# The last sequence of an attention stage: order of the down-row reads, PSUM banks, division and Silu table

## Chip, cores and metric

The kernel runs on one core of one Trainium2 chip. The metric is device microseconds for one execution of the whole program. PE is the tensor engine (TensorE), PEld its weight loads, ACT is ScalarE, DVE is VectorE, POOL is GpSimd, SP is the engine that here only issues DMAs.

## What is computed

x has 16 sequences of 256 tokens with 256 channels. Four blocks follow, each added to its input after a layer norm: causal attention with 16 heads, a feed-forward stage whose weights are rebuilt from spline control points, a gated linear attention, and the feed-forward stage again.

```python
x = x + attn_a(layernorm(x), Wq, Wk, Wv, Wo)        # 16 heads of 16, causal softmax
x = x + ffn(layernorm(x), gate_cp, up_cp, down_cp)  # down(silu(gate(x)) * up(x)), 1024 inner
x = x + attn_b(layernorm(x), Wq, Wk, Wog, Wig, g)   # gated linear attention
x = x + ffn(layernorm(x), gate_cp, up_cp, down_cp)
```

The change lies in the first block's last sequences and the first rows of the first feed-forward stage.

## The kernel before

Everything is fp32 kept as a high and a low part, so a projection is three matmuls (`mm3`, L414 to L416). Each engine has its own program, written out by hand, and runs it strictly in order; engines meet only at semaphores. `upto(s, b, k)` is the count that semaphore s has when step k of sequence b is done.

**Attention** runs in periods, one for each sequence b = 0 to 15. A period has eight steps p, each for a pair of heads. In step p PE makes the shifted scores of b (`shifted`, L870, into the double bank `pair_a`), then the plain scores of b + 1 (`scores` and `hide_future`, L839 and L851, into `pair_b`), of which DVE takes maxima (L1689). ACT takes the exponential (`exps`, L1314) from `pair_a`, POOL masks it (L660), and every second step PE weighs V with it (`weigh`, L884 and L888). `shifted(b, u, p)` waits until the exponential of step p - 1 has read `pair_a`.

The maxima become two rows of the operand that `shifted` reads: `turn_max` (PE, L858), `split_max` (DVE, L1702, L1704), and `max_rows(b, u, h)` (SP, L505), four DMAs of 4 KB, once for steps 0 to 3 (h = 0) and once for steps 4 to 7 (h = 1). `stack_half` (SP, L497), six DMAs of 128 KB, brings the other rows of a later sequence. The rest of a period finishes sequence b - 1: `turn_o` (L897), `divide` (DVE, L1711 and L1715), `turn_att` (L905), `copy_att` and `low_att` (L1326, L1722), `proj_out` and `residual` (L1728).

**The feed-forward stage (FFN)** works on eight groups of 512 tokens. For each group DVE takes statistics (L1829), ACT normalises into `xr` (L1433), PE turns it (`f1_turn`, two calls a group, L1071), ACT and DVE write high and low parts to `fs` (`f1_high_x` L1439, `f1_low_x` L1848), moments follow (`f1_moments`, `f1_high_moments` L1444, `f1_low_moments` L1853). SP stores these to `fx` in device memory (`f1_write_x`, four DMAs, `f1_write_moments`, two; L557 and L559) and reads them back in another layout to `stk` (`f1_read`, eight DMAs, L578). Then come eight steps m: gate (L1103) into `pair_a`, up (L1106) into `pair_b`, Silu on ACT (L1449), the product on DVE (`gated`, L1860), and from m = 3 on the down matmuls of step m - 3.

The first three groups' inputs are prepared inside attention's last periods. In the last period (b = 15) there are no scores of b + 1, so `pair_b` is free: the turns of groups 1 and 2 and the moments of group 1 use it. FFN group 0 also carries the end of sequence 15 (`last_attention`): turn_o at m = 0, division and turn_att at m = 1, proj_out at m = 2.

The **down weights** come from `wdx` in device memory by 16 DMAs (`load_down`, L526), eight in period 14 after `max_rows(14, 1)` and eight at its very end after the fx stores. In period 15 ACT makes their high part (`high_down`, L1362) and DVE the low part (`low_down`, L1823) in steps 2, 4, 6 and 7. All DMAs of SP are issued in the order of its program. Its period before:

```python
max_rows(b, u, 1)
if nxt2: stack_half(b + 2, u, 0)
if nxt and not nxt2: load_down(range(KG // 2))      # b = 14
if nxt: max_rows(b + 1, 1 - u, 0)
if nxt2: stack_half(b + 2, u, 1)
if nxt and not nxt2:                                # b = 14
    f1_write_x(0, 0); f1_write_moments(0, 0)
    load_down(range(KG // 2, KG))
```

`nxt`, `nxt2`, `nxt3` say whether sequences b + 1, b + 2, b + 3 exist.

## Time and profile before

| | us |
|---|---|
| median of three runs | 854.33 |
| their range | 853.58 to 856.82 |
| the profiled execution's span | 855.9 |
| PE, weight loads busy | 781.1, 661.1 |
| DVE, ACT, POOL busy | 629.3, 495.2, 236.7 |

No other time of the profiled execution is given than its span, the time from its first to its last instruction. The page cuts the span into 40 slices of 21.4 us; attention is slices 3 to 17, and the last sequence and the start of the FFN lie in slices 17 to 19, where PE has an 8 and the granted clock an 8. A row of a window gives its length, the busy us (and instructions) of PE, PEld, DVE, ACT and POOL, the granted clock, the busy share of the 16 DMA engines and GB/s. A window's granted clock is a mean: 1.00 is 2.4 GHz, 0.50 is 1.2 GHz. In a timeline the number in brackets is the idle time of the engine before the instruction, with what released it. PE's row of a matmul counts its modelled end, so starts are the better measure of its pace.

### The profile page before, as it was taken

What the parts mean: (1) busy time and instruction counts of PE and PEld (TensorE: products, weight loads), DVE (VectorE), ACT (ScalarE), POOL (GpSimd) and SP (SyncE); (2) the same over time, 40 slices, a digit from 0 to 9 for tenths busy, and PEclk for the clock granted to TensorE, in tenths of its full rate; (3) what the DMA queues carried; (4) which work ended last, traced back from release to release, by engine and by line L of the source; (5) the groups of instructions that cost most, each with busy time, mean ns of one, the idle gap of its engine ahead of it and who ended that gap; (6) DMA issues with size and microseconds to landing.
All of it is one profiled execution on the core that took longest, in us unless ns stands there. A gap on an engine that the chain in (4) does not pass through costs nothing.

```text
span 855.9 us, 19706 instructions
## 1 busy us (share of the span) xinstructions
PE 781.1 (91%) x6676; PEld 661.1 (77%) x6676; DVE 629.3 (74%) x1272; ACT 495.2 (58%) x967; POOL 236.7 (28%) x306
## 2 busy tenths in 40 slices
PE   4789899999999999869999999999999869999998
PEld 3667677777777777648889888888888849898887
DVE  7466777777777777736888767689887647887755
ACT  3146455555455556565666657588887736666643
POOL 2932223322323332311001001166666451000000
PEclk9669999999999999968999999999999988999999
DMA  5945766666666655575666640000033134777741
GB/s 182 112 79 79 147 89 97 97 94 90 88 95 97 96 87 78 159 262 174 254 237 233 243 163 2 1 2 1 1 134 149 37 120 162 256 257 272 263 156 50
DMA packets 70960, 111.16 MB, mean 130 GB/s; under 512 B 7061, under 2 KB 27958, under 8 KB 70854
## 3 DMA queue, kind: packets, MB, share of 16 engines
q1 hardware_dynamic: 70896, 110.35, 50.6%
q8 instruction: 35, 0.57, 0.3%
q14 instruction: 29, 0.24, 0.1%
HBM read 41.82 MB, written 42.81 MB: 99 GB/s over the span
## 4 chain that ended last, share of the span: by engine, by line
PE 48%; DVE 16%; issue 9%; ACT 8%; DMA 7%; SPq 7%; POOL 4%; ACTq 0%; DVEq 0%; POOLq 0%
PE bank L414 7%; PE bank L415 6%; PE bank L416 6%; DMA stk<-fx 5%; PE pair_a L870 4%; DVE inter L1860 4%; PE bank L884 4%; PE pair_b L839 3%; SPq L578 3%; PE pair_a L1156 2%; ACT in_hi L1457 2%; DVE in_lo L1865 2%; DVE spline L1937 2%; ACT gact L1449 2%; ACT xr L1433 2%
## 5 line engine op out<-in xcount | busy, mean ns | idle before, releaser
L414 PE MATMUL bank<-wd_hi,in_hi 128*128 128x256 f32 x512 | 146.4, 286 | 2.0 <-DVE X L1871 1.7
L416 PE MATMUL bank<-wd_hi,in_lo 128*128 128x256 f32 x512 | 145.5, 284 | 0.0
L415 PE MATMUL bank<-wd_lo,in_hi 128*128 128x256 f32 x512 | 145.3, 284 | 0.0
L1314 ACT ACTIVATE prob<-pair_a 128x768 f32<-128x768 f32 x128 | 103.7, 810 | 66.5 <-PE pair_a L870 65.5
L660 POOL TENSOR_SCALAR_AFFINE_SELECT prob<-prob 128x512 f32<-128x512 f32 x128 | 82.1, 641 | 212.8 <-ACT prob L1314 212.8
L1457 ACT ACTIVATE in_hi<-inter 128x512 fp32r<-128x512 f32 x128 | 80.7, 630 | 103.2 <-DVE inter L1860 97.6
L1865 DVE TENSOR_TENSOR in_lo<-inter,in_hi 128x512 fp32r<-128x512 f32 x128 | 89.0, 696 | 64.8 <-ACT in_hi L1457 63.4
L1689 DVE TENSOR_REDUCE mx<-pair_b 128x6 f32<-128x768 f32 x124 | 118.0, 952 | 24.1 <-PE pair_b L851 23.1
L414 PEld LDWEIGHTS bank<-wd_hi,in_hi 128*128 128x128 f32 x512 | 97.8, 191 | 7.1 <-issue 2.3
L415 PEld LDWEIGHTS bank<-wd_lo,in_hi 128*128 128x128 f32 x512 | 97.5, 190 | 4.8
L416 PEld LDWEIGHTS bank<-wd_hi,in_lo 128*128 128x128 f32 x512 | 97.5, 190 | 0.0
L1860 DVE TENSOR_TENSOR inter<-gact,pair_b 128x512 f32<-128x512 f32 x128 | 87.0, 680 | 6.3 <-ACT gact L1449 4.8
L1449 ACT ACTIVATE gact<-pair_a 128x512 f32<-128x512 f32 x128 | 74.5, 582 | 5.9 <-PE pair_a L1103 5.9
L870 PE MATMUL pair_a<-stack 50*128 50x256 f32 x512 | 66.6, 339 | 11.7 <-ACT prob L1314 7.7
L870 PEld LDWEIGHTS pair_a<-stack 50*128 50x128 f32 x512 | 39.8, 191 | 37.3 <-issue 14.8
L1103 PE MATMUL pair_a<-stk,cst 126*128 126x512 f32 x128 | 52.9, 413 | 11.2 <-DMA stk<-fx 6.1
L839 PE MATMUL pair_b<-stack 48*128 48x256 f32 x496 | 56.2, 304 | 5.2 <-DVE mx L1689 2.4
L712 POOL TENSOR_TENSOR frs<-fve,half_neg 128x4 f32<-128x4 f32 x16 | 16.1, 1008 | 144.2 <-DVE fve L1839 144.2
L1106 PE MATMUL pair_b<-stk,cst 126*128 126x512 f32 x128 | 53.9, 421 | 1.5 <-DVE inter L1860 1.5
L1302 ACT ACTIVATE stage<-bank 128x512 fp32r<-128x512 f32 x32 | 19.2, 599 | 56.2 <-PE bank L416 53.2
L839 PEld LDWEIGHTS pair_b<-stack 48*128 48x128 f32 x496 | 39.3, 192 | 12.5 <-DVE mx L1689 7.6
L884 PE MATMUL bank<-prob,V 128*32 128x256 f32 x512 | 42.7, 406 | 0.1
(226 smaller groups left out, 1960.9 us busy)
## 6 DMA issues: line engine op xcount, KB each, us to landing
stk<-fx SPq DMA_DIRECT2D x128, 252.0 KB
stack<-stage SPq DMA_DIRECT2D x192, 128.0 KB, 4.7
fx<-fs SPq DMA_DIRECT2D x32, 512.0 KB, 3.5
fx<-fs SPq DMA_DIRECT2D x32, 256.0 KB, 3.7
fx<-fs SPq DMA_DIRECT2D x16, 504.0 KB
fx<-fs SPq DMA_DIRECT2D x16, 252.0 KB
X<-in_attn_a_x SPq DMA_DIRECT2D x14, 256.0 KB, 5.0
result<-X SPq DMA_DIRECT2D x7, 512.0 KB, 8.1
```

The costliest lines, as they stand in the source:

```text
L414: pe.matmul(dst, l_hi, r_hi, start=first, stop=False)
L415: pe.matmul(dst, l_hi, r_lo, start=False, stop=False)
L416: return pe.matmul(dst, l_lo, r_hi, start=False, stop=last)
L660: pool.affine_select(out=diag, in_=diag, compare_op=ALU.is_ge, fill=0.0, base=0, pattern=[[0, 2], [0, 2], [1, P]], channel_multiplier=-1). ...
L839: pe.matmul(dst[:, n, at_col:at_col + S], stack[rows, u, h, p % PR, 0, P * t:P * t + P], stack[rows, u, h, p % PR, 1, :], start=(t == 1), ...
L870: i = pe.matmul(pair_a[:, n, at_col:at_col + S], stack[rows, u, h, p % PR, 1, P * t:P * t + P], stack[rows, u, h, p % PR, 0, :], start=Tru ...
L1314: act.activation(prob[:, p % 4], pair_a[:, :, P:4 * P], ACT.Exp, scale=DK ** -0.5).then_inc(a_e, 1)
L1449: act.activation(gact[:, m % 2, :], pair_a[:, m % 2, :], ACT.Silu).then_inc(f_.si, 1)
L1457: act.activation(in_hi[:, m % LAG, :], inter[:, m % 2, :], ACT.Copy).then_inc(f_.ih, 1)
L1689: dve.tensor_reduce(mx[:, h, :, p % PR, :], src[:, :, 0:3 * P].rearrange("p n (t k) -> p n t k", t=3), AX.X, ALU.max).then_inc(a_mx, 1)
L1860: dve.tensor_tensor(inter[:, m % 2, :], gact[:, m % 2, :], pair_b[:, m % 2, :], ALU.mult).then_inc(f_.up, 1)
L1865: dve.tensor_tensor(in_lo[:, m % LAG, :], inter[:, m % 2, :], in_hi[:, m % LAG, :].bitcast(F32), ALU.subtract).then_inc(f_.il, 1)
```

## The change

On SP, the first eight down reads move from period 14 (after `max_rows(14, 1)`) to the end of period 13, ahead of `max_rows(14, 1)`. The second eight, and `f1_write_x(0, 0)`, move ahead of `max_rows(15, 0)`. `f1_write_moments(0, 0)` stays behind it.

In period 15 shifted scores go to `pair_a` in even steps and to `pair_b` in odd ones, and wait only for the exponential of step p - 2. So the turns and moments of groups 1 and 2 leave `pair_b` for single banks (`bank_y`, `bank_p`, `bank_t`) at steps 0, 3 and 5, each with waits for the bank's former reader. `high_down` moves from ACT to DVE, both down parts at steps 2 to 5. ACT runs a Silu of one element a partition right after the last exponential, which loads Silu's table there. `divide(15, 1)` moves from m = 1 to m = 0 of FFN group 0, ahead of the first `gated`.

```diff
 (SP, period)
                 if nxt and not nxt2:
-                    load_down(range(KG // 2))
+                    load_down(range(KG // 2, KG))
+                    f1_write_x(0, 0)
                 if nxt:
                     max_rows(b + 1, 1 - u, 0)
                 if nxt2:
                     stack_half(b + 2, u, 1)
+                if nxt2 and not nxt3 and b == B - 3:
+                    load_down(range(KG // 2))
...
                 if nxt and not nxt2:
-                    f1_write_x(0, 0)
                     f1_write_moments(0, 0)
-                    load_down(range(KG // 2, KG))
 (PE, shifted)
-                pe.wait_ge(a_e, upto(a_e, b, p))
+                last = isinstance(b, int) and b == B - 1
+                pe.wait_ge(a_e, upto(a_e, b, p - 1 if last and p else p))
+                dst = pair_b if last and p % 2 else pair_a
 (PE, period)
+                    if p == 0 and not nxt:
+                        pe.wait_ge(a_mx, upto(a_mx, B - 1, NP))
                     shifted(b, u, p)
...
                     if p == 2 and prev:
                         pe.wait_ge(a_at, upto(a_at, b - 1, 1))
+                        if not nxt:
+                            pe.wait_ge(f_.xl, upto(f_.xl, 1, 1))
                         turn_o(b - 1, 1)
...
                         elif nxt:
                             pe.wait_ge(f_.ml, upto(f_.ml, 0, 1))
+                        else:
+                            pe.wait_ge(f_.xl, upto(f_.xl, 2, CT))
                         pe.wait_ge(a_res, upto(a_res, b - 2, 1))
                         proj_out(b - 1)
                     if not nxt:
                         if p == 0:
-                            pe.wait_ge(a_mx, upto(a_mx, B - 1, NP))
-                        if p in (1, 5):
-                            if p == 5:
-                                pe.wait_ge(f_.ml, upto(f_.ml, 1, 1))
-                            for c in range(CT):
-                                f1_turn(1 + p // 4, c, pair_b[:, c, :])
+                            pe.wait_ge(a_at, upto(a_at, B - 2, 1))
+                            f1_turn(1, 0, bank_y)
+                            pe.wait_ge(a_res, upto(a_res, B - 3, 1))
+                            f1_turn(1, 1, bank_p)
                         if p == 3:
-                            f1_moments(1, pair_b[:, 0, :])
+                            f1_moments(1, bank_p)
+                        if p == 5:
+                            pe.wait_ge(a_atl, upto(a_atl, B - 2, 1))
+                            f1_turn(2, 0, bank_t)
+                            pe.wait_ge(f_.ml, upto(f_.ml, 1, 1))
+                            f1_turn(2, 1, bank_p)
 (ACT, period)
                     exps(b, p)
+                    if p == NP - 1 and not nxt:
+                        act.activation(silu_first[:, :], quarter[:, :], ACT.Silu)
...
-                        if p in (1, 7):
-                            for c in range(CT):
-                                f1_high_x(1 + p // 4, c, pair_b[:, c, :])
-                        if p == 3:
-                            f1_high_moments(1, pair_b[:, 0, :])
+                        if p == 1:
+                            f1_high_x(1, 0, bank_y)
+                            f1_high_x(1, 1, bank_p)
                         if p == 4:
                             f1_normalise(2)
-                        if p in (2, 4, 6, 7):
-                            high_down((p - 1) // 2)
+                        if p == 6:
+                            f1_high_x(2, 0, bank_t)
+                            f1_high_x(2, 1, bank_p)
...
                             copy_att(b - 1)
+                        if not nxt:
+                            f1_high_moments(1, bank_p)
 (DVE, period; low parts of groups 1 and 2 at p = 1, 3, 6 in the same banks)
-                        if p in (2, 4, 6, 7):
-                            low_down((p - 1) // 2)
+                        if p in (2, 3, 4, 5):
+                            high_down(p - 2)
+                            low_down(p - 2)
 (DVE)
+            def high_down(n):
+                dve.wait_ge(s_wd, 256)
+                rows = slice(2 * n, 2 * n + 2)
+                dve.tensor_copy(wd_hi[:, rows, :], wd_lo[:, rows, :].bitcast(F32)).then_inc(s_wdh, 1)
 (DVE, last_attention)
-                if m == 1:
+                if m == 0:
                     divide(B - 1, 1)
```

## Rows read from the trace of the kernel before

**Rows 1.** Windows: each engine's busy us (instructions), granted clock, DMA share, GB/s.

```profile
364.00:366.00 2.00, 0.00 (x0) 0.00 (x0) 0.00 (x0) 0.58 (x2) 0.00 (x0) 1.00 0.26 93
366.00:368.00 2.00, 1.11 (x8) 0.73 (x12) 0.94 (x2) 2.00 (x5) 0.64 (x1) 0.69 1.01 378
380.00:382.00 2.00, 1.33 (x15) 0.72 (x8) 1.89 (x4) 1.23 (x2) 0.00 (x0) 0.90 0.58 226
386.00:388.00 2.00, 0.59 (x4) 0.18 (x2) 2.00 (x5) 1.60 (x3) 0.00 (x0) 0.81 0.61 169
```

**Rows 2.** Timeline of PE: start, us, line, tiles, count, idle before; last sequence.

```profile
353.89 0.50 PE L870 MATMUL pair_a<-stack 50*128 50x256 f32 x4
...
354.77 0.40 PE L888 MATMUL bank<-prob,V 128*32 128x128 f32 x8
...
356.04 1.04 PE L1071 MATMUL pair_b<-ident,xr 128*128 128x128 f32 x8
...
366.89 0.79 PE L870 MATMUL pair_a<-stack 50*128 50x256 f32 x4 [3.21 <-ACT prob L1314]
...
381.34 0.50 PE L1103 MATMUL pair_a<-stk,cst 126*128 126x512 f32 x1 [0.67 <-DVE fs L1848]
```

**Rows 3.** Timeline of ACT, then of DVE; last sequence.

```profile
358.99 1.08 ACT L1439 ACTIVATE fs<-pair_b 128x512 fp32r<-128x512 f32 x2 [2.25 <-DMA fx<-fs]
359.96 0.82 ACT L1314 ACTIVATE prob<-pair_a 128x768 f32<-128x768 f32 x1
365.42 0.63 ACT L1362 ACTIVATE wd_hi<-wd_lo 128x512 fp32r<-128x512 f32 x1 [4.64 <-DMA wd_lo<-wdx]
...
368.43 2.07 ACT L1433 ACTIVATE xr<-X,fnmr,frs 128x256 f32<-128x256 f32 x4
...
381.37 1.28 ACT L1449 ACT_TABLE_LOAD   x1
...
359.62 1.29 DVE L1848 TENSOR_TENSOR fs<-pair_b,fs 128x512 fp32r<-128x512 f32 x2 [2.05 <-ACT fs L1439]
```

**Rows 4.** Timeline of PE's weight loads: shifted(14, 4) and shifted(15, 4).

```profile
342.95 0.30 PEld L870 LDWEIGHTS pair_a<-stack 50*128 50x128 f32 x4 [0.19 <-DMA stack<-mrow]
...
366.86 0.53 PEld L870 LDWEIGHTS pair_a<-stack 50*128 50x128 f32 x4 [3.60 <-DMA stack<-mrow]
```

**Rows 5.** Timeline of SP's queue, issues only; periods 13 to 15.

```profile
333.90 4.89 SPq L497 DMA_DIRECT2D stack<-stage  x6
339.24 2.56 SPq L505 DMA_DIRECT2D stack<-mrow  x4
341.84 2.90 SPq L526 DMA_DIRECT2D wd_lo<-wdx  x8
...
357.44 4.71 SPq L526 DMA_DIRECT2D wd_lo<-wdx  x8
362.20 2.44 SPq L505 DMA_DIRECT2D stack<-mrow  x4
364.75 0.39 SPq L557 DMA_DIRECT2D fx<-fs  x1
```

**Rows 6.** Windows as in rows 1: stack copies, down reads, reads of stk.

```profile
339.00:340.00 1.00, 1.00 (x22) 0.57 (x18) 1.00 (x2) 0.33 (x1) 0.51 (x1) 1.00 1.04 123
347.00:348.00 1.00, 1.00 (x9) 0.81 (x5) 0.63 (x5) 0.67 (x1) 0.17 (x1) 1.00 0.56 76
372.00:373.00 1.00, 1.00 (x7) 0.67 (x5) 0.00 (x0) 0.19 (x1) 0.64 (x1) 0.50 0.58 211
```

**Rows 7.** DMA issues of 325 to 395: count and KB each.

```profile
stk<-fx SPq DMA_DIRECT2D x16, 252.0 KB
...
wd_lo<-wdx SPq DMA_DIRECT2D x16, 64.0 KB
```

**Rows 8.** Timeline of PE: start of the FFN, and its first down matmul.

```profile
385.37 0.66 PE L905 MATMUL bank<-ident,att 128*128 128x128 f32 x4 [2.38 <-DVE att L1715]
...
394.02 0.30 PE L414 MATMUL bank<-wd_hi,in_hi 128*128 128x256 f32 x1
```

More of the change, by code:

```diff
@@ L188, in build @@
         quarter = sb("quarter", [P, 1], F32)
+        silu_first = sb("silu_first", [P, 1], F32)
         cst = sb("cst", [NFX, 2, MT, P], F32R)
@@ L869, in shifted @@
                         rows = slice(HALF * n, HALF * n + K_ST)
-                        i = pe.matmul(pair_a[:, n, at_col:at_col + S], stack[rows, u, h, p % PR, 1, P * t:P * t + P],
+                        i = pe.matmul(dst[:, n, at_col:at_col + S], stack[rows, u, h, p % PR, 1, P * t:P * t + P],
                                       stack[rows, u, h, p % PR, 0, :], start=True, stop=True,
@@ L1264, in _ @@
             weigh(B - 1, 1, NP - 2)
-            pe.wait_ge(f_.xl, upto(f_.xl, 2, CT))
             pe.wait_ge(s_ce, 6)
@@ L1313, in exps @@
                 act.wait_ge(a_pv, upto(a_pv, b, p - 3))
-                act.activation(prob[:, p % 4], pair_a[:, :, P:4 * P], ACT.Exp,
+                src = pair_b if isinstance(b, int) and b == B - 1 and p % 2 else pair_a
+                act.activation(prob[:, p % 4], src[:, :, P:4 * P], ACT.Exp,
                                scale=DK ** -0.5).then_inc(a_e, 1)
@@ L1357, in spread_rows @@
                     act.activation(wdn[:, 0, :, 0:1], wdn[:, 0, :, D:D + 1], ACT.Copy).then_inc(s_wdn, 1)
-            def high_down(n):
-                act.wait_ge(s_wd, 256)
-                rows = slice(2 * n, 2 * n + 2)
-                act.activation(wd_hi[:, rows, :], wd_lo[:, rows, :].bitcast(F32), ACT.Copy).then_inc(s_wdh, 1)
             act.wait_ge(s_const, 5)
@@ L1807, in period @@
                     if not nxt:
-                        if p in (1, 7):
-                            for c in range(CT):
-                                f1_low_x(1 + p // 4, c, pair_b[:, c, :])
-                        if p == 3:
-                            f1_low_moments(1, pair_b[:, 0, :])
                         if p == 0:
                             f1_stats(2)
-                        if p in (2, 4, 6, 7):
-                            low_down((p - 1) // 2)
+                        if p == 1:
+                            f1_low_x(1, 0, bank_y)
+                            f1_low_x(1, 1, bank_p)
+                        if p == 3:
+                            f1_low_moments(1, bank_p)
+                        if p in (2, 3, 4, 5):
+                            high_down(p - 2)
+                            low_down(p - 2)
+                        if p == 6:
+                            f1_low_x(2, 0, bank_t)
+                            f1_low_x(2, 1, bank_p)
             attention = period
+            def high_down(n):
+                dve.wait_ge(s_wd, 256)
+                rows = slice(2 * n, 2 * n + 2)
+                dve.tensor_copy(wd_hi[:, rows, :], wd_lo[:, rows, :].bitcast(F32)).then_inc(s_wdh, 1)
             def low_down(n):
```

## The prediction, on record before the changed kernel was run

> **What bounds the kernel now.** I read the page's slices of the span first: the tensor engine (PE) is nearly always busy in the attention periods and again once the first feed-forward stage (FFN) runs, so little can be won there. The one hole is the last sequence, b = 15, from its first shifted scores at 353.89 to the first gate matmul at 381.34, 27.45 us [rows 2]. Its windows show what goes wrong: PE does nothing at all from 364 to 366, the granted clock is 1.00 until then and 0.69 over the next window, so 0.50, that is 1.2 instead of 2.4 GHz, from about 366.8 on; in 380 to 382 it is 0.90, so it came back at about 380.4 [rows 1]. The timelines of ACT and PE then name the waits. ACT stood 2.25 us for the landing of `f1_write_x(0, 0)` before it could copy the next FFN input, and 4.64 us for the down rows; PE, in order behind the exponentials, stood 3.21 us, and the matmuls after it run at half rate [rows 2, 3]. The third thing is the queue of SP: the rows of maxima (`max_rows`), the down rows and the fx stores share one queue, and `max_rows(14, 1)` is landed only 0.19 us after PE wants it at 342.95 [rows 4]. That one decides this forecast.
>
> **The change part by part.**
>
> *The last sequence on PE, clock at 2.4 GHz; t = 0 is its first shifted scores.* A set of shifted scores and a weighing take 1.28 us together (353.89 to 354.77 + 0.40), which I split 0.43 and 0.85; eight turns take 1.04, one exponential 0.82, two copies to fs 1.08 on ACT and 1.29 on DVE, a normalisation 2.07 [rows 2, 3]. I follow the new order by these. p = 0: shifted(0), weigh, f1_turn(1, 0) and (1, 1), to 2.25. p = 1: shifted(1) goes to pair_b and no longer waits for exps(0); turn_max to 3.1. DVE then writes the maxima's rows by 4.0; exps(1) ends at 3.6, high_x at 4.6, low_x at 5.4. The wait for the fx store is gone, because that store is issued a period earlier. p = 2 to 3: weigh(0) must wait for mask(1) until 4.5, turn_o to 5.9, division on DVE to 6.7, turn_att and the moments to 8.6. p = 4 to 5: shifted, weigh, shifted to 10.3; then PE waits for ACT's normalisation, which ends at 12.2. p = 6 to 7: the turns, shifted, weigh, turn_o to 15.7, shifted(7) to 16.15; proj_out now waits for low_x(2), which stands behind divide(15, 0) on DVE, until 17.7; proj_out and the last weighing end at 20.1. The eight down copies are now on DVE, each pair of copy and subtraction at most 1.35 us (a subtraction of this shape takes half of the 1.29 us above; a copy of it has no row on DVE and lies between nothing and the same): they fill DVE's gap from 6.7 to 14, and cost nothing as long as divide(15, 0) at 15.8 finds DVE free. ACT loses 4 x 0.63 us of copies that were beside PE's waits [rows 3].
>
> *A new wait takes the place of the old ones.* The first gate needs all eight reads of stk. Before, `f1_write_x(1, 1)` was issued at 364.75 and the reads right behind it [rows 5]. They move 8 x 252 KB at 211 GB/s with 0.58 of the DMA engines busy [rows 6, 7], so 9.5 us, behind about 4 us of fx stores; with a little over 1 us at each end that is 15.8 us from the first store to the last landing, and 364.75 + 15.8 = 380.5 was just hidden under the gate at 381.34. Now the store is issued when low_x(1) is done (5.4) and SP is through with `max_rows(15, 1)` (4.05 + 2.44 = 6.5), and 6.5 + 15.8 = 22.3. PE is ready at 20.1, so the gate comes at 22.4. Gain in this stretch: 27.45 - 22.4 = 5.05 us. Bounds: 7.3 (the reads come in time) and 4 (some idle time lowers the clock again).
>
> *The down rows read sooner, and what they are moved past.* Eight reads are now issued at the end of the queue's work of period 13, at 338.8 (333.90 + 4.89), ahead of `max_rows(14, 1)`, which was issued at 339.24 [rows 5]. Their issue alone takes 2.90 us (clear queue) to 4.71 (busy queue), and shifted(14, 4), which wants those rows, stands at the head of PE with everything behind it: a delay of 2.5 us is the least (the old issue at 339.24 becomes 341.7). But the transfers are slower than the issue. In the old order these same eight kept 0.56 of the DMA engines busy and moved 76 GB/s in a window of their stretch [rows 6]: 8 x 64 KB [rows 7] is 6.9 us at that rate. The stretch as a whole, six windows from 343 to 349, is a little faster, so I take 6.1. In the new order they queue behind stack_half(15, 1), which keeps all DMA engines busy in 339 to 340 and ends at about 340.7, so they move until 346.8. If the rows of maxima lie on the same DMA engines in order, they come after: 346.8 + 1.7 = 348.5, that is 5.6 us after 342.95. The upper bound is 6.2 (the queue's slower issues added), the lower 2.5.
>
> The share alone does not say whether the four small rows meet the eight down rows. The Trainium skill ("DMA: Bandwidth & Descriptors", in its part on how many engines k a DMA gets) says that a copy is split over the largest count up to 16 that divides both outer dimensions and that these are the lowest-numbered engines; by that the maxima's four are a part of the down rows' eight, ring order holds, and this speaks against the change: 5.6 us rather than 2.5. No row here names an engine. I take 5.6, because the one place where maxima's rows followed down rows before (issued from 362.20 for 2.44 us) released PE at 366.86, 2.2 us after their last issue against 1.15 us at 342.95 [rows 4, 5]; that is a weak witness, since an exponential ended at about the same time. All of these transfers also lie in the one hardware queue of the page.
>
> *The clock.* PE would be idle from about 342.8 to 348.5. Before, 3.2 us of idle time were enough for a fall to 0.50 [rows 1, 2], so here it falls too, in a stretch in which PE never waits. The fall at 366.8 lasted until 380.4; the next one came at about 387.2 (0.81 in 386 to 388), after a wait of 2.38 us, and was over at 394.02, where a matmul of 256 columns takes 0.30 us [rows 1, 8]. So a fall here lasts 6.8 to 13.6 us. Of the new one, the first 2 us fall on idle time; 4.6 us at half rate cost 2.3 us, 11 cost 5.5. I take 2.5, less 0.4 us of small waits that disappear at half rate. Nothing (no fall) is the other bound.
>
> *Second store moved.* `f1_write_x(0, 0)` and the other eight down reads now stand ahead of `max_rows(15, 0)`. That waits for the maxima of DVE anyway, which come some 8 us later now, and by my count the transfers ahead (6.1 us of reads from 347, then 4 us of stores) end at 357.5, before it lands at 361. Cost nothing; if the cover goes, up to 1 us.
>
> *The start of the FFN.* Division is ahead of the first gated product, and the Silu table (1.28 us) is loaded in ACT's wait for the last weighing [rows 3]. silu(0) comes 0.6 us sooner, but divide (0.7 us) now stands before gated(0), which so starts where it did. turn_att, which PE waited 2.38 us for, is 1.9 us sooner [rows 8]. low_att however keeps its place behind the second pair of statistics on DVE: seven steps at 0.6 us, started 0.6 us sooner. So proj_out comes 0.5 to 0.6 us sooner, not 2. From the gate to the first down matmul took 12.7 us [rows 2, 8], 6.8 of them at half clock; if the clock stays up it is 9.3. Gain 0 to 3.4, I take 0.9, since PE is idle 2.3 us before the gate and 2.5 us before proj_out and the clock probably falls again.
>
> *Sum:* +5.6 + 2.5 - 0.4 - 5.05 - 0.9 = +1.75 us. From the first down matmul on PE is busy almost without a gap and the shift passes to the end. The sum is made against the profiled execution, whose span is 855.9 us, 1.6 over the median of 854.33 and inside the runs shown (853.58 to 856.82); I carry the difference over to the median: 856.1.
>
> **The rivals.**
> *A: the maxima's rows pass the down reads* (other DMA engines, or the issue alone counts). For it: only 0.58 of the engines are busy. Against it: one queue, and the landing in period 15. The stall is 2.5 to 3.7 us and the clock costs 0 to 2.3: the sum is 2.5 + 0 - 5.05 - 3.4 = -6 at best and 3.7 + 2.3 - 0.4 - 5.05 - 0.9 = -0.4 at worst. Time 848.4 to 854, middle 850.5.
> *B, slower: the clock stays down.* After the stall in period 14 PE at 1.2 GHz is given work with many small tiles, as from 366.8 to 380.4, and the clock does not rise before the last sequence starts. Then the clock costs 5.5 us, the steps before 6.5 in the last sequence 1 us more, and the FFN's start gives nothing: 5.6 + 5.5 + 1 - 5.05 = +7, time 861. It decides from about 356: a clock still at 0.50 there is this case.
> *C: the reads of stk come in time after all,* or the change does not shorten the last sequence as said because a DVE wait (divide ahead of low_x) moves the store or the last projection. The first gives 2.3 us more (854), the second 2 us less (858). Both stay within 0.5%.
>
> **How the numbers follow.** Forecast with C: 0.62 (sum from -0.6 to +4). A: 0.22. B: 0.16. 0.5% is 4.3 us, about what a measurement of this kernel can tell from no change. More than that faster is most of A's better half: 0.15. More than that slower is B and an edge of the forecast: 0.20. Within it 0.65. The range leaves out the ends of A and B: 849.5 to 861.0.
>
> **What would show it.** In the profile after: the first down read issued at about 338.8; PE idle before shifted(14, 4) for 5 to 6 us with the release by the maxima's rows, and the clock at 0.50 soon after; the last sequence 22 to 23 us long at full clock with no wait for wd_lo and a wait for stk of about 2 us before the first gate; the table load ended before that gate; turn_att close behind up(1) and proj_out some 6 us after the gate. The forecast is wrong if the wait in period 14 is under 3 us, if the clock does not fall there or stays down, or if the gate does not wait for stk.

## The result, and the profile after

| | median, us | runs shown | ratio to before, 95% interval |
|---|---|---|---|
| before | 856.51 | 853.13 to 860.57 (12) | |
| changed | 861.49 | 858.09 to 868.00 (12) | 1.0068 [1.0044, 1.0093] |

The change costs 5.0 us, 0.7%. The profiled execution took 868.0 us, the longest of the twelve, with a span of 866.3 against 855.9 before. The medians and ratios below leave out a few executions in a slower state of the chip (865.95 and 875.27 us, and three of about 1411).

The difference of the spans must first be cleared of something that has nothing to do with the change. The windows below (length, busy us of PE, PEld, DVE, ACT, POOL, granted clock, DMA share, GB/s) show PE fully busy at 0.50, so at 1.2 GHz, early in attention, where both kernels run the same instructions:

```profile
74.00:86.00 12.00, 12.00 (x78) 9.79 (x77) 2.97 (x5) 6.73 (x17) 1.28 (x2) 0.50 0.44 55
86.00:88.00 2.00, 2.00 (x18) 1.77 (x19) 1.73 (x4) 0.81 (x1) 0.30 (x1) 0.73 0.00 0
```

The trace of before has no such stretch there. With it, period 14 starts at 341.03 instead of 334.89, 6.1 us late. All that follows is therefore measured from the start of period 14, and a time of before is compared after adding 6.1. That the 5.1 us found in this way agree with the 5.0 us of the medians supports the reckoning.

**The stretch that changed.** Times are starts of weight loads in PE's timeline: shifted(14, 0), shifted(14, 4), shifted(15, 0), first gate, first down matmul.

| | (14,0) to (14,4) | to (15,0) | last sequence, to gate | gate to down | all | after it |
|---|---|---|---|---|---|---|
| before | 8.06 | 10.93 | 27.46 | 12.26 | 58.71 | 462.3 |
| changed | 16.97 | 12.90 | 23.08 | 10.90 | 63.85 | 461.4 |
| difference | +8.91 | +1.97 | -4.38 | -1.36 | +5.14 | -0.9 |

The first column is a stall. PE's weight loads in the changed kernel, at shifted(14, 4) and at the first gate (start, us, engine, line, tiles, count, idle time and what ended it):

```profile
358.00 0.50 PEld L874 LDWEIGHTS pair_a<-stack 50*128 50x128 f32 x4 [9.09 <-DMA stack<-mrow]
...
393.98 0.29 PEld L1116 LDWEIGHTS pair_a<-stk,cst 126*128 126x128 f32 x1 [0.38 <-issue]
```

The wait of 0.19 us for the same maxima's rows [rows 4] has become 9.09. At the gate PE now hardly waits. SP's issues in the changed kernel say where the rows stood:

```profile
340.05 4.85 SPq L498 DMA_DIRECT2D stack<-stage  x6
344.94 2.95 SPq L527 DMA_DIRECT2D wd_lo<-wdx  x8
347.94 2.56 SPq L506 DMA_DIRECT2D stack<-mrow  x4
350.55 2.93 SPq L527 DMA_DIRECT2D wd_lo<-wdx  x8
...
377.44 0.39 SPq L559 DMA_DIRECT2D fx<-fs  x1
...
380.12 6.48 SPq L580 DMA_DIRECT2D stk<-fx  x8
```

The rows of (14, 1) were issued by 350.5, 2.6 us later than in [rows 5] once the shift of 6.1 is taken off. The other 6.3 us of the 8.9 are landing: 7.5 us from the end of the issue to PE's start, against 1.15 before. What the DMA engines and the clock did meanwhile, in windows of the changed kernel:

```profile
349.00:353.00 4.00, 0.14 (x2) 0.00 (x0) 1.83 (x5) 0.70 (x2) 0.17 (x1) 1.00 0.57 66
352.00:354.00 2.00, 0.00 (x0) 0.00 (x0) 0.00 (x0) 0.00 (x0) 0.00 (x0) 0.83 0.57 66
354.00:358.00 4.00, 0.00 (x0) 0.00 (x0) 0.00 (x0) 0.00 (x0) 0.00 (x0) 0.50 1.02 243
...
362.00:364.00 2.00, 2.00 (x15) 1.81 (x13) 0.67 (x6) 0.24 (x1) 0.00 (x0) 0.61 0.52 144
364.00:366.00 2.00, 2.00 (x19) 1.49 (x16) 0.96 (x1) 1.06 (x2) 0.78 (x2) 1.00 0.53 205
```

The down reads move 66 GB/s at a share of 0.57, not the 76 at 0.56 of [rows 6]; why they are slower here is not shown. The clock falls in the stall and is back at 2.4 GHz at about 363.5, some 5.5 us after PE goes on; that is the second column. Four more places of PE in the last sequence and the FFN's start (start, us, line, tiles, count, idle and releaser):

```profile
383.14 1.10 PE L1084 MATMUL bank<-ident,xr 128*128 128x128 f32 x8 [1.78 <-ACT xr L1444]
...
389.68 0.58 PE L415 MATMUL bank<-wo_hi,attT_hi 128*128 128x256 f32 x1 [1.28 <-DVE fs L1868]
...
396.30 0.66 PE L909 MATMUL bank<-ident,att 128*128 128x128 f32 x4 [0.34 <-DVE att L1726]
400.22 0.35 PE L415 MATMUL bank<-wo_hi,attT_hi 128*128 128x256 f32 x1 [2.80 <-DVE attT_lo L1733]
```

### The profile page after: what moved, and what is told of

The parts are those of the page before. It is cut to its first block, busy times and chain, and to the rows that moved or that the text cites. A ratio compares the mean times of both kernels' runs of the same rounds, so it can differ in the third digit from the quotient of the medians.

```text
span 866.3 us, 19708 instructions
## 1 busy us (share of the span) xinstructions
PE 784.8 (91%) x6676; PEld 663.5 (77%) x6676; DVE 632.0 (73%) x1276; ACT 493.9 (57%) x964; POOL 237.4 (27%) x306
## 4 chain that ended last, share of the span: by engine, by line
PE 47%; DVE 17%; issue 11%; ACT 9%; DMA 5%; SPq 5%; POOL 4%; ACTq 1%; DVEq 1%; POOLq 0%
PE bank L415 7%; PE bank L417 5%; PE bank L416 5%; DVE inter L1880 5%; PE pair_a L874 4%; PE bank L888 4%; PE pair_b L841 3%; DMA stk<-fx 3%; ACT gact L1460 3%; PE pair_a L1169 2%; ACT in_hi L1468 2%; DVE in_lo L1885 2%; DVE spline L1957 2%; ACT xr L1444 2%; SPq L580 2%
## 5 line engine op out<-in xcount | busy, mean ns | idle before, releaser
L1327 ACT ACTIVATE prob<-pair_a 128x768 f32<-128x768 f32 x124 | 100.5, 810 | 73.5 <-PE pair_a L874 72.6
L841 PEld LDWEIGHTS pair_b<-stack 48*128 48x128 f32 x496 | 40.5, 196 | 12.2 <-DVE mx L1700 7.8
```

The costliest lines, as they stand in the source:

```text
L841: pe.matmul(dst[:, n, at_col:at_col + S], stack[rows, u, h, p % PR, 0, P * t:P * t + P], stack[rows, u, h, p % PR, 1, :], start=(t == 1), ...
L1327: act.activation(prob[:, p % 4], src[:, :, P:4 * P], ACT.Exp, scale=DK ** -0.5).then_inc(a_e, 1)
```

## The experiments

The theory after the result, Q: the rows of maxima stand behind the down reads, and these move slowly; the reads of stk set the length of the last sequence, and the edits on PE, ACT and DVE do little. The other versions below keep the whole computation; only order, issuer and timing differ. Ratios are to the kernel before, run on the same chip, with a 95% interval.

**1. SP's order alone.** The kernel before with only the new order of SP (the first two hunks of the change's diff), nothing on the other engines.

> The kernel before with the new order of SP's queue alone (down reads 0 to 7 at the end of period 13, reads 8 to 15 and the first fx store ahead of max_rows(15, 0)); all other engines as before. Theory Q (the maxima's rows of sequence 14 wait in the queue behind the down reads): PE stands 8 to 9.5 us before shifted(14, 4), the clock falls to 0.50 there, and since the down rows are then early the last sequence loses its waits for them and for the fx store (about 5 us back). Time 4 to 8 us over the kernel before. Rival C (the loss comes from the new work in the last sequence: DVE copies, a later wait for stk): no stall in period 14, time at or below the kernel before.

859.40 us, ratio 1.0040 [1.0014, 1.0067]. SP's queue, PE's weight load at shifted(14, 4), and PE's first gate:

```profile
337.41 2.94 SPq L526 DMA_DIRECT2D wd_lo<-wdx  x8
340.40 2.56 SPq L505 DMA_DIRECT2D stack<-mrow  x4
...
350.45 0.50 PEld L871 LDWEIGHTS pair_a<-stack 50*128 50x128 f32 x4 [9.35 <-DMA stack<-mrow]
...
384.84 0.47 PE L1104 MATMUL pair_a<-stk,cst 126*128 126x512 f32 x1 [2.63 <-DMA stk<-fx]
```

The stall is there in full, 9.35 us. The last sequence is 22.08 us long, shorter even than with all edits (23.08). So SP's order alone makes both the loss and the gain; the two ratios, 1.0040 and 1.0068, have overlapping intervals. Here the gate does wait for stk, 2.63 us in PE's timeline, as the prediction had it for the full change.

**2. Is it what stands ahead, or behind?** The changed kernel with the second eight reads and the fx store put back behind the rows of (15, 0).

```diff
-                if nxt and not nxt2:
-                    load_down(range(KG // 2, KG))
-                    f1_write_x(0, 0)
...
                 if nxt and not nxt2:
+                    f1_write_x(0, 0)
                     f1_write_moments(0, 0)
+                    load_down(range(KG // 2, KG))
```

> The changed kernel with only the first eight down reads moved; the second eight and the first fx store are back behind max_rows(15, 0). Whether these, issued right after max_rows(14, 1), lengthen the stall. If only what stands ahead in the queue counts (Q): the stall before shifted(14, 4) stays near 8.9 us. If traffic issued behind also slows the rows' landing (Q2): the stall falls to 5.5 to 7 us, the size forecast. The second eight land late again, so DVE waits for down rows in the last sequence; time 3 to 9 us over the kernel before.

863.44 us, ratio 1.0089 [1.0058, 1.0120]. PE still waited 8.00 us, so the traffic behind the rows makes only about 1 us of the 9. The last sequence is 26.68 us long here, since the waits of before are back in it (ACT, then DVE):

```profile
375.11 1.09 ACT L1449 ACTIVATE fs<-bank 128x512 fp32r<-128x512 f32 x2 [1.98 <-DMA fx<-fs]
...
381.55 0.43 DVE L1837 CAST wd_hi<-wd_lo 128x512 fp32r<-128x512 f32 x1 [3.18 <-DMA wd_lo<-wdx]
```

This version also gives the cleanest picture of how long eight reads take in the new place, because nothing follows them. Its windows:

```profile
346.00:347.00 1.00, 1.00 (x12) 0.83 (x12) 0.29 (x2) 0.60 (x1) 0.00 (x0) 1.00 0.87 95
347.00:348.00 1.00, 1.00 (x14) 0.64 (x10) 1.00 (x3) 0.81 (x1) 0.00 (x0) 1.00 0.66 73
...
349.00:353.00 4.00, 0.00 (x0) 0.00 (x0) 1.42 (x4) 0.34 (x1) 0.00 (x0) 0.90 0.57 65
353.00:354.00 1.00, 0.00 (x0) 0.00 (x0) 0.00 (x0) 0.00 (x0) 0.00 (x0) 0.50 0.57 66
354.00:355.00 1.00, 0.00 (x0) 0.00 (x0) 0.00 (x0) 0.00 (x0) 0.00 (x0) 0.50 0.23 25
355.00:356.00 1.00, 0.00 (x0) 0.00 (x0) 0.00 (x0) 0.00 (x0) 0.00 (x0) 0.50 0.00 0
```

In the two windows before these, with the stack copies, the share is 1.09; what stands above 0.57 in the first two windows puts their end at 346.75 ((0.30 + 0.09) / 0.52 after 346). From there the reads run at 0.57 until 354.4 (0.23 / 0.57 into that window), 7.65 us, and PE starts at 356.46, 2.1 us behind their end. At 65 GB/s 64 KB take 1.0 us. In the kernel before, the same eight reads, issued behind the rows, took about 6 us (343 to 349, 90 GB/s at a share of 0.58). What makes them slower ahead of the rows stays open.

**3. No down read ahead of the rows.** The changed kernel with each eight one place later: the first behind the rows of (14, 1), the second behind those of (15, 0).

```diff
-                    load_down(range(KG // 2, KG))
+                    load_down(range(KG // 2))
                     f1_write_x(0, 0)
...
-                if nxt2 and not nxt3 and b == B - 3:
-                    load_down(range(KG // 2))
...
                 if nxt and not nxt2:
+                    load_down(range(KG // 2, KG))
                     f1_write_moments(0, 0)
```

> The changed kernel with no down read ahead of max_rows(14, 1): the first eight behind it, then the first fx store, max_rows(15, 0), then the second eight, then the fx store of moments. Q: no stall before shifted(14, 4) (0.2 us as in the kernel before), the clock stays at 1.00 in period 14, a gain of 8 to 11 us against the changed kernel; the rows of maxima for shifted(15, 0) now lie behind eight reads and a store and may cost 0 to 3 us. Time 2 to 6 us under the kernel before. Rival C: within 2 us of the changed kernel.

855.22 us, ratio 0.9989 [0.9960, 1.0018]: the loss is gone, and so is the gain; the 2 to 6 us under before were not reached. shifted(14, 4) waits 0.19 us as before, but PE then waited at shifted(15, 0), for rows that SP issued behind the reads and the fx store. SP's issues, then PE:

```profile
345.96 2.91 SPq L527 DMA_DIRECT2D wd_lo<-wdx  x8
349.11 0.39 SPq L558 DMA_DIRECT2D fx<-fs  x1
...
354.34 2.45 SPq L506 DMA_DIRECT2D stack<-mrow  x4
...
360.40 0.50 PE L873 MATMUL pair_a<-stack 50*128 50x256 f32 x4 [2.33 <-issue]
```

The trace names no releaser here ("issue"); that the rows were it is inferred from their order. The last sequence was 27.11 us. No instruction of ACT or DVE in it waits for the down reads or the fx store. What its trace shows is half clock for most of it, in 363 to 372 after that wait and again from 376.5 on, after the one for the normalisation:

```profile
363.00:372.00 9.00, 8.36 (x44) 5.47 (x44) 4.47 (x9) 3.90 (x6) 3.08 (x5) 0.50 0.47 176
```

**4. Half as many ahead.** The changed kernel with four reads ahead of the rows (`KG // 4`) and twelve behind; one profile and no interval.

> The changed kernel with four instead of eight down reads ahead of max_rows(14, 1); the other four join the eight behind it. If the stall is the transfer time of what stands ahead in the queue (Q), at the 1.0 to 1.2 us a read that the stall of 8.9 us suggests, it falls by 4 to 4.5 us, to 4.5 to 5 us. If traffic issued behind counts much (Q2: twelve reads and a store instead of eight and a store), it falls by less than 2 us.

PE's weight load at shifted(14, 4):

```profile
346.78 0.50 PEld L874 LDWEIGHTS pair_a<-stack 50*128 50x128 f32 x4 [5.11 <-DMA stack<-mrow]
```

From shifted(14, 0) to (14, 4) it took 12.99 us: 4.93 over before, against 8.91 with eight. The four reads between are worth (8.91 - 4.93) / 4 = 1.0 us each, the same figure that the rate gives. So the stall grows by 1.0 us with each read ahead, and 4.93 - 4 x 1.0 = 0.9 us of it come besides, about what experiment 2 gives for the traffic behind the rows.

**5. Another queue.** The first eight reads issued by ACT, whose DMAs have a queue of their own (q10 on this version's page, q1 for SP), in steps 0 to 3 of period 14, so around SP's issue of the rows; otherwise the changed kernel, one profile and no interval.

```diff
 (SP, period)
-                if nxt2 and not nxt3 and b == B - 3:
-                    load_down(range(KG // 2))
 (ACT, period)
                     exps(b, p)
+                    if nxt and not nxt2 and p < 4:
+                        act.wait_ge(s_wdx, 32)
+                        for k in (2 * p, 2 * p + 1):
+                            act.dma_start(wd_lo[8 * k:8 * k + 8, :, :].bitcast(F32),
+                                          wdx[64 * k + 1:64 * k + 65].rearrange("(m j) d -> j m d", j=8)
+                                          ).then_inc(s_wd, 16)
```

> The changed kernel with the first eight down reads issued by ACT, two behind each of the exponentials 0 to 3 of period 14, so at about the same time but in ACT's DMA queue. Q (order within SP's one queue makes the wait): the stall before shifted(14, 4) is under 2 us. If instead the DMA engines are simply full with down reads, whoever issues them: 3 us or more. ACT's own issue time may cost some 3 us in period 14 either way.

It did not help: PE's weight load waited 7.77 us for the rows. Theory Q as I had put it, a matter of order within SP's one queue, fell. Two causes were left: the reads hold the rows up from another queue, or the eight reads and the fx stores that SP issues behind the rows do.

**6. Another queue, and nothing behind.** As 5, but the second eight reads go two at a time in periods 4 to 7, and the fx store waits until after the rows of (15, 0).

> As other_queue, the first eight reads of wd rows issued by ACT on its own queue just before the maxima's rows of (14,1), but nothing issued behind these rows by SP: the second eight reads go two at a time in periods 4 to 7, and the store of fx waits for max_rows(15,0). If the stall of 7.5 us in other_queue came of the eight reads themselves (they share DMA engines with the maxima's rows whoever issues them), a wait of 5 to 8 us stays ahead of shifted(14,4). If it came of what SP put behind the rows (eight reads and two stores), the wait is under 2 us. The time of one look isn't used; the stall is.

ACT's and SP's issues, and PE, in this version:

```profile
337.96 0.89 ACTq L1388 DMA_DIRECT2D wd_lo<-wdx  x2
340.88 0.63 ACTq L1388 DMA_DIRECT2D wd_lo<-wdx  x2
...
338.69 23.03 SPq L506 DMA_DIRECT2D stack<-mrow  x8
...
349.51 0.79 PE L873 MATMUL pair_a<-stack 50*128 50x256 f32 x4 [7.05 <-DMA stack<-mrow]
```

(The SP row joins the four rows of (14, 1), issued from 338.69, with the four of (15, 0), which come after a long wait.) The windows of that time:

```profile
344.00:346.00 2.00, 0.00 (x0) 0.00 (x0) 0.41 (x1) 0.00 (x0) 0.00 (x0) 1.00 0.57 66
346.00:348.00 2.00, 0.00 (x0) 0.00 (x0) 0.00 (x0) 0.00 (x0) 0.00 (x0) 0.51 0.55 66
348.00:350.00 2.00, 0.49 (x4) 0.49 (x6) 0.00 (x0) 0.00 (x0) 0.00 (x0) 0.50 0.06 8
```

The stall stays, 7.05 us on PE. Nothing but the eight reads is under way, on another queue and with 0.57 of the DMA engines busy, and PE is released a good 1 us after they are through, although the last two were issued only while SP was issuing the rows. So the first of the two causes holds: the rows land after the down reads that were issued just ahead of them or beside them, whoever issued these. Reads issued right behind them do not hold them up like this (1.15 us from issue to PE's start in the kernel before).

The Trainium skill has a rule for this ("DMA: Bandwidth & Descriptors", section "Queues, rings and completion order"): the write that announces a DMA's end lands only after every earlier write of that DMA engine, across its queues. The traces agree with it (7.77 and 7.29 us of waiting in PE's weight loads, across two queues), but no row names a DMA engine, and whether the rows' data or only their announcement came late was not told apart.

**7. The reads spread out.** The changed kernel with the sixteen down reads two at a time in periods 4 to 11, right behind the rows of (b, 1). (SP's periods are written out, so that b is a number in each.)

```diff
                 max_rows(b, u, 1)
+                if 4 <= b < 12:
+                    load_down(range(2 * b - 8, 2 * b - 6))
...
                 if nxt and not nxt2:
-                    load_down(range(KG // 2, KG))
                     f1_write_x(0, 0)
...
-                if nxt2 and not nxt3 and b == B - 3:
-                    load_down(range(KG // 2))
...
-            run_periods(sp, period)
+            for n in range(B):
+                period(n, n // 2, n % 2, prev=n > 0, nxt=n < B - 1, nxt2=n < B - 2, nxt3=n < B - 3)
```

> The changed kernel with the sixteen down reads issued two at a time in periods 4 to 11, right after max_rows(b, 1), where the queue has some 3 us with nothing to issue; SP's periods are written out instead of looped. Q: no stall in period 14, last sequence about 22 to 23 us as in the changed kernel, start of the FFN about 11 us; sum -4.4 - 1.6 = 6 us under the kernel before (3 to 8). If the reads delay stack rows in their periods, some 0.5 us in each of eight periods is lost, and it comes out equal to the kernel before.

849.89 us, ratio 0.9917 [0.9883, 0.9951], faster than both kernels. The stretch is 52.23 us (8.08 + 10.94 + 22.45 + 10.76). The stall is gone, and two reads of some 2 us find room in each earlier period: period 14 starts at 335.08 us, against 334.89 before. The same kernel, run once more beside number 10:

> The spread version again on the same chip as reads_split, to compare the two: 5 to 8 us under the kernel before, last sequence about 22.4 us.

849.97 us, 0.9916 [0.9891, 0.9942]: it repeats.

**8. The same without the other edits.** The kernel before, with the reads spread as in 7 and the fx store ahead of the rows of (15, 0); one bank pair for shifted, copies on ACT, late table load and late division as before.

```diff
                 max_rows(b, u, 1)
+                if 4 <= b < 12:
+                    load_down(range(2 * b - 8, 2 * b - 6))
...
                 if nxt and not nxt2:
-                    load_down(range(KG // 2))
+                    f1_write_x(0, 0)
...
                 if nxt and not nxt2:
-                    f1_write_x(0, 0)
                     f1_write_moments(0, 0)
-                    load_down(range(KG // 2, KG))
```

> The kernel before with only the queue changed: down reads two at a time in periods 4 to 11 and the first fx store ahead of max_rows(15, 0); shifted scores in pair_a alone, down copies on ACT, division and Silu table where they were. Theory R (the last sequence now ends with the reads of stk, not with PE): last sequence 22.1 to 22.8 us, start of the FFN 11 to 12 us, time 5 to 6.5 us under the kernel before, so within 1 us of the spread version with all other parts. Rival P (the two pairs of banks shorten the last sequence): last sequence 25 us or more, time 3 us or less under the kernel before.

851.04 us, 0.9902 [0.9863, 0.9942], and a stretch of 52.45: the same as 7. SP's issues, then the start of PE's proj_out, its last weighing and first gate:

```profile
358.83 0.39 SPq L557 DMA_DIRECT2D fx<-fs  x1
...
361.52 6.84 SPq L578 DMA_DIRECT2D stk<-fx  x8
...
369.23 0.39 PE L414 MATMUL bank<-wo_hi,attT_hi 128*128 128x256 f32 x1
...
371.47 0.40 PE L889 MATMUL bank<-prob,V 128*32 128x128 f32 x8
375.19 0.77 PE L1104 MATMUL pair_a<-stk,cst 126*128 126x512 f32 x1 [3.32 <-DMA stk<-fx]
```

PE is through with attention at 371.9, 19 us into the last sequence, without the two pairs of banks, and then stands 3.3 us for the reads of stk. With the pairs PE's path is not shorter but longer. The same places in version 7:

```profile
372.73 0.38 PE L415 MATMUL bank<-wo_hi,attT_hi 128*128 128x256 f32 x1 [1.57 <-DVE fs L1868]
...
376.58 0.76 PE L1116 MATMUL pair_a<-stk,cst 126*128 126x512 f32 x1 [0.33 <-issue]
```

proj_out writes `bank_p`, which one turn of group 2 now uses, so it waits for `low_x(2)` and starts 18.6 us into the last sequence, against 16.7 here. The last weighing starts at 21.5 to 22.5 us in the changed kernel and versions 7 and 9, and at 18.9 and 19.1 in versions 8 and 1, which have one pair. So with the pairs PE comes to the gate about when the reads of stk land, and nothing of the shorter waits is left.

**9. The FFN's start.** Version 7 without the early Silu table and with the division at m = 1 again.

> The spread version without the early Silu table and with division back at m = 1. Forecast for these two together was 0.6 us of proj_out's start (up to 3.4 with the clock). Expected: first gate to first down matmul 11.3 to 12.7 us against 10.8, time 0.5 to 2 us over the spread version; if they are worth nothing, the same head of 10.8.

851.51 us, 0.9909 [0.9871, 0.9947]. From gate to first down matmul 11.81 us instead of 10.76; in the whole time no difference can be seen. Since version 8 has the late forms too and took 10.86, even the 1 us is not safely theirs.

**10. Two of the eight reads of stk earlier.** Version 7 with two of these reads ahead of the rows of (15, 1).

```diff
+                if not nxt:
+                    sp.wait_ge(s_zeros, 32)
+                    sp.wait_ge(a_stp, upto(a_stp, B - 2, NP))
+                    f1_read(0, 0, range(2))
                 max_rows(b, u, 1)
...
-            f1_read(0, 0)
+            f1_read(0, 0, range(2, MT))
```

> The spread version with two of the eight reads of stk for FFN group 0 issued ahead of max_rows(15, 1), before the second fx store. Theory R: the reads of stk end the last sequence, so it gets shorter by two reads' 2.3 us until PE's own 20.1 us end it: 20.1 to 21 us against 22.45, with a small risk that the rows for shifted(15, 4) come late; time 1 to 2.3 us under the spread version. If PE's path is what ends it, the last sequence stays at 22.4.

847.91 us, 0.9911 [0.9882, 0.9940], against 849.97 and 0.9916 for version 7 beside it: a difference is not shown. The expected shortening of the last sequence is not there: 23.64 us. PE's weight load now waited 1.17 us for the maxima's rows that the two reads delay, and at the gate only the 0.38 us that the other traces with the pairs have too: PE's own path is the limit, as it nearly was in version 7.

**11. The same on top of version 8,** with the early table and the early division.

> The kernel before with SP's reads of wd rows two at a time (as spread_before), and three more edits: two of the eight reads of stk issued ahead of max_rows(15,1), the Silu table loaded at the first of shifted's waits, and the division ahead of the first gate. Shifted keeps its four banks in a row and the fp32 additions, without the changed kernel's two pairs. Theory R (in spread_before PE stood 3.56 us ahead of the gate because the reads of stk ended the last sequence, while PE was ready about 19 us in): with two reads gone earlier the wait shrinks and PE's own path ends the sequence, 20 to 21.5 us instead of 22.6; the head falls from 10.9 to 10 to 10.9; the time is 7 to 10 us under before, 0 to 2.5 us under spread. Theory P (the pairs of banks shorten PE's path): without them PE is ready no earlier than 23.6 us, what reads_split took with them, and the last sequence is 23.6 us or longer; the time is 4 to 7 us under before.

848.98 us, ratio 0.9933 [0.9904, 0.9963], 5.7 us under before by the ratio. The last sequence took 22.69 us, between what the two theories gave (20 to 21.5, or 23.6 and more), so neither number was met; the time lies in what theory P gave (4 to 7 us under before), not in R's 7 to 10. PE in it, at shifted(15, 4), at a turn, and at the first gate:

```profile
362.63 0.50 PE L876 MATMUL pair_a<-stack 50*128 50x256 f32 x4 [0.91 <-DMA stack<-mrow]
...
366.09 1.06 PE L1077 MATMUL pair_b<-ident,xr 128*128 128x128 f32 x8 [1.55 <-ACT xr L1441]
...
376.33 0.50 PE L1109 MATMUL pair_a<-stk,cst 126*128 126x512 f32 x1 [1.19 <-DVE fs L1856]
```

The wait for stk is gone, and in its place are one for the rows, one for ACT, after which matmuls ran at half rate, and one for DVE, which still reads `pair_b`. Saving at the reads of stk is given back at once. The FFN's start took 9.04 us here, at a granted clock of 1.00 throughout:

```profile
376.00:378.00 2.00, 1.64 (x8) 1.07 (x8) 1.30 (x4) 0.72 (x2) 0.00 (x0) 1.00 0.52 198
378.00:382.00 4.00, 1.12 (x6) 0.76 (x6) 3.96 (x9) 2.71 (x5) 0.00 (x0) 1.00 0.94 328
382.00:386.00 4.00, 3.76 (x24) 3.43 (x25) 3.71 (x12) 1.44 (x3) 1.25 (x4) 1.00 0.58 218
```

## Why the prediction was right or wrong

The forecast of 856.1 us was 5.4 too low, and the measured 861.49 lies just above the range's end of 861.0. About 2.2 of the 5.4 come from the base: three runs had given 854.33 for the kernel before, twelve gave 856.51. The sum itself missed 3.4 us, by these steps.

- *The stall in period 14: 5.6 forecast, 8.9 measured. This is the step that failed, by its size.* That the rows land behind the eight reads was right. By the windows of experiment 2 four of its terms were short. The start: the stack copies end 6.15 us into period 14, not 5.8, +0.35. The reads: windows of before gave 6.1 us for eight, and in the new place they take 7.65, +1.55; the forecast carried their old rate over to it. The landing: PE starts 2.05 us after the reads' end, not 1.7, +0.35. And the reads and stores issued behind the rows, which I had counted as harmless, add 1.1 (16.97 against 15.87 us from shifted(14, 0) to (14, 4), one profile each). That makes the 3.3. The 1.7 us of landing had been set between the 1.15 and the 2.2 us of its rows, without a row of its own. My upper bound of 6.2 took only the slower issue into account and no error in the rate; that is why the range was too short on this side.
- *The reason given, ring order in one queue, was too narrow.* Experiments 5 and 6 show the same wait with the reads in another queue. The forecast did not depend on it, but a repair built on it (issue by ACT) would have failed.
- *The clock: 2.5 - 0.4 = 2.1 forecast, 1.97 measured.* It fell in the stall, at about 353.3 (0.83 in 352 to 354), and stayed down until about 363.5, 10 us, within the 6.8 to 13.6 us given for such a fall; 4.7 us of it fell on idle time, not 2.
- *The last sequence: 22.4 us forecast, 23.08 measured,* a gain of 4.4 instead of 5.05, within its bounds. The single steps held: the store of group 1 was issued at 377.44, 6.5 us in, as forecast; the wait for ACT's normalisation ended at 12.2 (383.14 - 370.90), as forecast; the projection's wait for low_x(2) ended at 18.8 instead of 17.7. But PE was ready only at about 22.7, not 20.1: 1.1 us of that is the later projection, the rest the clock, which was at 0.50 again when proj_out and the last weighing ran. So the wait of 2 us for stk, a sign the prediction had made its own test, did not show in this trace. It shows where one pair of banks lets proj_out start earlier: 2.63 us in experiment 1, 3.32 in experiment 8. From the store's issue to the gate it took 15.85 and 16.36 us there, forecast 15.8 (its 9.5 us for eight reads of stk are 9.8 by its own figures).
- *Where the gain came from.* I had followed PE's new path in every step and priced the pairs of banks, the copies on DVE and the shorter waits into it. Experiments 1 and 8 have none of these and reach 22.08 and 22.58 us. What was needed was that the second eight down reads and the first fx store are out of the way, so that ACT no longer waits 2.25 and 4.64 us for them [rows 3] and SP comes to the reads of stk earlier; with both put back, experiment 2 has such waits again and 26.68 us. Which of the two counts for more was not told apart. The prediction's own sentence that stk ends the sequence says it; I did not draw the conclusion that the rest of the change can gain nothing.
- *DVE's copies:* 0.42 us each for 128 x 512, 1.1 for a pair with its subtraction, inside the 1.35 allowed (one subtraction of the four took 1.00). No wait of PE was traced to them.
- *The second store moved: at no cost, as forecast,* as long as the stall is there to cover it. Without the stall and with eight reads ahead of the store it costs 2.3 us on PE, more than the 1 us I named (experiment 3); without reads ahead of it, nothing (7 and 8).
- *The FFN's start: -0.9 forecast, -1.36 measured.* turn_att came close behind (0.34 us of wait, rows above) and the projection still waited 2.80 us for attT_lo, as forecast. The trace with a full clock gave 9.04 us where I had said 9.3.
- *The rivals.* A (rows pass the reads) fell. B gave the measured time, 861 (its sum of +7.05 makes 861.4, just outside the stated range), but not for its reason, and that the times agree is luck: the clock rose at about 363.5, before the last sequence began at 370.90, so what B added for the clock was not paid; a larger stall took its place. Of C, the second half came in part: the last projection started 1.1 us later than forecast, held up by DVE, and the last sequence gave 0.67 us less than forecast, not 2. The first half did not appear.
- *The chances.* "Within 0.5%" had 0.65 and "slower" 0.20; measured is 0.68% slower. With a stall of 8.9 in the sum it would have been +5.1 us and slower the likeliest, so the one mis-sized term would have changed this too.

Left open: why the down reads move more slowly ahead of the rows than behind them; whether the two pairs of banks would pay if proj_out did not wait for `bank_p` (no version has this); and whether the rows' data or their announcement is late. Also unexplained is why PE's clock was at 1.2 GHz in 74 to 86 of the changed kernel's trace while PE was busy all the time; traces of the other versions have such stretches at other places or none.

## What to carry to other kernels

Before moving a bulk read ahead of a small transfer that an engine waits for, price the whole read as a delay of the small one, at the slowest rate that a trace shows for it, add something for what is issued behind, and don't count on a share of idle DMA engines or on another issuer's queue: here neither helped. Data that is needed once and late is best read in small pieces in periods that have room, as in version 7, which brought 0.8%. And if the chain's last wait is for a transfer, try the reordering of transfers alone first: here it was all of the gain, and the edits on PE, ACT and DVE added nothing that could be measured in the time. A bank that a new step takes over has a next writer, and that writer's wait belongs in the path too: with proj_out's wait for `bank_p`, the last weighing came no earlier but 2.4 us or more later.

## What the runs showed of the hardware that I had not expected

- Eight reads of 64 KB down rows, issued ahead of the maxima's rows, move 65 to 66 GB/s at a share of 0.57 with nothing beside them, 1.0 us each; issued behind the rows, in the kernel before, they moved 90 GB/s at 0.58 on the mean of 343 to 349.
- Four transfers of 4 KB on SP's queue land only after eight reads on ACT's queue: 7.3 to 7.8 us of waiting.
- A copy with rounding of 128 x 512 fp32 takes 0.42 us on DVE, the subtraction of the same shape 0.69.
- ACT's table load took 1.28 us and the next activation started right behind it, in the changed kernel:

```profile
389.27 1.28 ACT L1387 ACT_TABLE_LOAD   x1
390.57 0.20 ACT L1387 ACTIVATE silu_first<-quarter 128x1 f32<-128x1 f32 x1
```
